# A Perceiver-style block: the values product of the self-attentions over both batches of a tile at once

## The reference

```python
# mla: q and k through Gelu and rotation, causal; ffn: not causal; attn: causal
scores = jnp.einsum('bhqd,bhkd->bhqk', q, k) * scale
attn   = jax.nn.softmax(scores, axis=-1)
out    = jnp.einsum('bhqk,bhkd->bhqd', attn, v)      # the values product
x      = x + out.reshape(b, s, E) @ wo               # (+ bo)
```

## Time and profile before

| what | value |
|---|---|
| median of 3 runs | 1062.91 us (1062.78 to 1072.04) |
| span of the profiled execution, first to last instruction | 1060.4 us |
| median less that span | 2.5 us |
| TensorE busy | 1019.5 us, 96% |
| VectorE, ScalarE, GpSimd busy | 647.4, 469.6, 243.5 us |
| self-attentions with values products | 362 to 513 us and 900 to 971 us |

### The profile page before, as it was taken

The page is one execution under the profiler, slowest core; times in us unless marked ns, Lnnn a source line. Parts: engine busy times, 40 slices in busy tenths (PEclk is TensorE's granted clock), DMA queues, the critical chain, the costliest instruction groups (busy, mean ns, idle before and its releaser), DMA issues.

```text
span 1060.4 us, 27662 instructions
## 1 busy us (share of the span) xinstructions
PE 1019.5 (96%) x11767; PEld 879.2 (83%) x11767; DVE 647.4 (61%) x1399; ACT 469.6 (44%) x863; POOL 243.5 (23%) x381
## 2 busy tenths in 40 slices
PE   5999999999999999999899999997999999999998
PEld 5888888888888787887689999996888888887887
DVE  5645645545333555776869999986667663355242
ACT  3333333333333556543156677762534433464232
POOL 2311211211111133442414444422211100011000
PEclk9999999999999999999889999999999999999999
DMA  9400000000000630220136557612111002000000
GB/s 306 140 2 21 21 2 21 2 1 1 2 1 2 227 123 3 81 101 13 43 79 239 198 199 257 239 61 90 41 38 47 12 2 72 3 2 2 1 20 20
DMA packets 55401, 72.54 MB, mean 68 GB/s; under 512 B 8488, under 2 KB 48624, under 8 KB 54640
## 3 DMA queue, kind: packets, MB, share of 16 engines
q1 hardware_dynamic: 53744, 66.59, 18.8%
q0 software_dynamic: 1536, 4.20, 1.3%
HBM read 59.76 MB, written 11.01 MB: 67 GB/s over the span
## 4 chain that ended last, share of the span: by engine, by line
PE 87%; DVE 7%; ACT 3%; issue 2%; DMA 1%; POOL 0%; DVEq 0%; ACTq 0%; POOLq 0%
PE ps L624 9%; PE ps L639 9%; PE ps L2321 8%; PE ps L2337 7%; PE ps L2684 5%; PE ps L1512 4%; PE ps L608 3%; PE ps L656 3%; PE ps L1430 3%; PE ps L1146 3%; PE ps L578 3%; PE ps L676 2%; PE ps L1469 2%; PE ps L1529 2%; PE ps L1081 2%; PE ps L1071 2%
## 5 line engine op out<-in xcount | busy, mean ns | idle before, releaser
L379 POOL TENSOR_TENSOR rn_tmp<-rn_cur,eps 128x1 f32<-128x1 f32 x48 | 14.1, 294 | 358.9 <-DVE rn_cur L373 358.7
L767 ACT ACTIVATE x0pT<-ps 128x512 f32<-128x512 f32 x64 | 38.3, 598 | 123.6 <-PE ps L639 123.6
L2321 PE MATMUL ps<-moe_xT_hi,ew_1hi 128*128 128x256 f32 x240 | 69.9, 291 | 2.3 <-DVE moe_xT_lo L2471 2.3
L2337 PE MATMUL ps<-ew_2hi,eh_hi 128*128 128x256 f32 x240 | 69.3, 289 | 2.5 <-DVE eh_lo L2479 2.5
L2321 PE MATMUL ps<-moe_xT_lo,ew_1hi 128*128 128x256 f32 x240 | 69.0, 288 | 0.0
L2321 PE MATMUL ps<-moe_xT_hi,ew_1lo 128*128 128x256 f32 x240 | 69.0, 287 | 0.0
L2477 DVE CAST eh_hi<-eh 128x512 fp32r<-128x512 f32 x60 | 61.1, 1018 | 11.0 <-ACT eh L2383 10.9
L2337 PE MATMUL ps<-ew_2hi,eh_lo 128*128 128x256 f32 x240 | 67.0, 279 | 0.0
L2337 PE MATMUL ps<-ew_2lo,eh_hi 128*128 128x256 f32 x240 | 66.9, 279 | 0.0
L876 DVE TENSOR_TENSOR x0A_lo<-ps,x0A_hi 128x512 fp32r<-128x512 f32 x64 | 41.1, 685 | 31.7 <-ACT x0A_hi L758 31.7
L2684 PE MATMUL ps<-f,ffw 128*128 128x512 f32 x256 | 59.1, 391 | 0.8 <-issue 0.6
(11 more groups left out here) (340 smaller groups left out, 2846.2 us busy)
## 6 DMA issues: line engine op xcount, KB each, us to landing
ew<-L_ffn_W_dram SPq DMA_DIRECT2D x30, 1024.0 KB, 7.2
x0cin<-ctx_dram SPq DMA_DIRECT2D x8, 512.0 KB, 4.2
x1cin<-ctx_dram SPq DMA_DIRECT2D x8, 512.0 KB, 4.0
moe_out<-moe_y SPq DMA_DIRECT2D x15, 256.0 KB, 7.8
xg<-moe_in SPq DMA_DIRECT2D x14, 256.0 KB, 7.8
moe_in<-padneg SPq DMA_DIRECT2D x3, 1024.0 KB, 12.4
maskrow<-mask_BxS_ik_dram SPq DMA_DIRECT2D x2, 1024.0 KB, 8.2
x0wk<-L_xattn_Wkv_dram SPq DMA_DIRECT2D x1, 1024.0 KB, 7.7
```

The lines of the kernel that those rows point to most:

```text
L767: nc.scalar.activation(g.pT[:, u, :], ps[:, S_BANK[u % 2], :], ACT.Exp, scale=64.0 ** -0.5).then_inc(C0.exp, 1)
L2321: last = nc.tensor.matmul(ps[:, n % 3, j * BT:j * BT + BT], w[b % 2][:, i, f * P:f * P + P], v[b % 2][:, i, :], start=(i == 0 and m == 0), ...
L2337: last = nc.tensor.matmul(ps[:, O_BANK[b % 2] + c, 0:D], v[n % 3][:, j * BT + c * P:j * BT + c * P + P], w[b % 2][:, f, :], start=(f == 0 ...
```

## The change

The values of an item lie in g.v as a block diagonal: for each head 2 x 18 columns, in which the keys of batch b fill only the columns of block b, and the other block holds zeros. One matmul then takes all 128 partitions of pT (both batches' keys) and 36 columns. Its output has the 64 queries of the head on 64 partitions, and both batches beside each other in the columns. The two halves of the output partitions hold heads j and 8 + j in place of the two batches. An item has 16 such matmuls, in two halves of 8. The zeros and ones come from a small tile "frame", filled once by VectorE and copied by GpSimd into the three buffers of v before each stage; the copies of v out of PSUM become two instructions of 64 partitions, and wait for that. The reciprocals, the scaled result and the transposed copy follow the new order of heads. Since v is larger, ln_st, hot_too and one eh_lo buffer lie elsewhere.

```diff
+        frame = sb("frame", [P, 2 * XVW])
...
-            v = [sb(f"sa_v{i}", [P, H, XVW]) for i in range(3)]
+            v = [sb(f"sa_v{i}", [P, H, 2, XVW]) for i in range(3)]
...
@@ self_tables(dve), in the first cross-attention
+            for b in range(2):
+                half = slice(64 * b, 64 * b + 64)
+                nc.vector.memset(frame[half, (1 - b) * XVW:(1 - b) * XVW + XVW], 0.0)
+                nc.vector.memset(frame[half, b * XVW:b * XVW + 16], 0.0)
+                last = nc.vector.memset(frame[half, b * XVW + 16:b * XVW + XVW], 1.0)
+            last.then_inc(SA.frame, 1)
@@ pool_x0(pool), loop over t and u
                     clip(t, u)
+                    if t == T - 1 and u == 4:
+                        value_frame(pool)
@@ pe_self
-            def fill_pv(n, hf):
-                if hf == 0:
+            def fill_pv(n, half):
+                if half == 0:
                     pe.wait_ge(SA.exp, n + 1)
+                    pe.wait_ge(SA.v_frame, 3 * span + 3)
                     RS.wait_emptied(pe, n, "v")
                     RS.wait_free(pe, n, "pv")
-                for hd in range(8 * hf, 8 * hf + 8):
-                    r, par = hd // 2 % 4, hd % 2
-                    for b in range(2):
-                        rows_b = slice(64 * b, 64 * b + 64)
+                for j in range(4 * half, 4 * half + 4):
+                    r, par = divmod(j, 2)
+                    for hf in range(2):
                         at_p = hf * P + par * N
-                        last = nc.tensor.matmul(RS.bank(n, "pv")[rows_b, hd * XVW:hd * XVW + XVW], g.pT[rows_b, r, at_p:at_p + N], g.v[n % 3][rows_b, hd, :],
-                                                start=True, stop=True, skip_group_check=True)
-                if hf == 1:
+                        last = nc.tensor.matmul(RS.bank(n, "pv")[64 * hf:64 * hf + 64, 2 * j * XVW:2 * j * XVW + 2 * XVW], g.pT[:, r, at_p:at_p + N],
+                                                g.v[n % 3][:, 8 * hf + j, :, :].rearrange("p b d -> p (b d)"), start=True, stop=True, skip_group_check=True)
+                if half == 1:
                     last.then_inc(SA.fill, 1)
@@ act_self (and the same on VectorE in dve_self)
             def v(n):
                 RS.wait_filled(act, n, "v")
-                nc.scalar.activation(g.v[n % 3][:, :, 0:16], RS.bank(n, "v")[:, 0:D].rearrange("p (h d) -> p h d", h=H), ACT.Copy).then_inc(SA.by_act, 1)
+                act.wait_ge(SA.v_frame, 3 * span + 3)
+                for b in range(2):
+                    half = slice(64 * b, 64 * b + 64)
+                    last = nc.scalar.activation(g.v[n % 3][half, :, b, 0:16], RS.bank(n, "v")[half, 0:D].rearrange("p (h d) -> p h d", h=H), ACT.Copy)
+                last.then_inc(SA.by_act, 1)
@@ attT(n)
-                bank = RS.bank(n, "T")
+                bank = RS.bank(n, "T")[:, 0:D].rearrange("p (b k n) -> p k b n", b=2, k=KD)
+                attT_b = g.attT[:, :, :].rearrange("p k (b n) -> p k b n", b=2)
...
-                    last = nc.scalar.activation(g.attT[:, :, :], bank[:, 0:D].rearrange("p (k n) -> p k n", k=KD), ACT.Copy)
+                    last = nc.scalar.activation(attT_b, bank, ACT.Copy)
@@ self_begin
-            for i in range(3):
-                nc.vector.memset(SB.v[i][:, :, 16:XVW], 1.0)
@@ attend(n)
-                nc.vector.reciprocal(g.rinv[:, :], pv[:, :, 16]).then_inc(SA.rinv, 1)
+                nc.vector.reciprocal(rinv, pv[:, :, :, 16]).then_inc(SA.rinv, 1)
                 dve.wait_ge(SA.rinv, n + 1)
-                nc.vector.tensor_tensor(g.att[:, :].rearrange("p (h d) -> p h d", h=H), pv[:, :, 0:16],
-                                        g.rinv[:, :].rearrange("p (h o) -> p h o", o=1).broadcast_to((P, H, 16)), ALU.mult).then_inc(SA.by_dve, 1)
+                nc.vector.tensor_tensor(g.att[:, :].rearrange("p (b j d) -> p j b d", b=2, j=8), pv[:, :, :, 0:16],
+                                        g.rinv[:, :].rearrange("p (j b o) -> p j b o", b=2, o=1).broadcast_to((P, 8, 2, 16)), ALU.mult).then_inc(SA.by_dve, 1)
@@ new, called by pool_x0 and pool_x1
+        def value_frame(pool):
+            pool.wait_ge(SA.frame, 1)
+            for i in range(3):
+                nc.gpsimd.tensor_copy(SB.v[i][:, :, :, :].rearrange("p h b d -> p h (b d)"),
+                                      frame[:, :].rearrange("p (o e) -> p o e", o=1).broadcast_to((P, H, 2 * XVW))).then_inc(SA.v_frame, 1)
```

More of the change, by code:

```diff
@@ L99, in build @@
         wg = sb("wg", [P, KD, P])
-        ln_st = sb("ln_st", [P, 5, 6])
         ln_mv = sb("ln_mv", [P, 5, 2])
@@ L178, in build @@
             wo = sb("x0wo", [P, 8, D])
+            ln_st = sb("ln_st", [P, 5, 6])
         at[0] = mark
@@ L215, in build @@
         b2 = sb("b2", [P, D])
-        eh_lo_at = at[0]
-        eh_lo = [sb("eh_lo2", [P, 512], F32R)]
         hot = [nc.alloc_sbuf_tensor_at(f"hot{i}", [P, BT], F32, offset=o) for i, o in enumerate(
-            [xg_at + 4 * D * i for i in (0, 1, 2, 3, 4, 5, 8, 9, 10, 11)])]
-        hot_too = nc.alloc_sbuf_tensor_at("hot_too", [P, BT], F32, offset=eh_lo_at)
+            [xg_at + 4 * D * i for i in (0, 1, 2, 3, 4, 5, 8, 9)])]
+        hot_too = nc.alloc_sbuf_tensor_at("hot_too", [P, BT], F32, offset=xg_at + 4 * D * 10)
         slot_no = nc.alloc_sbuf_tensor_at("slot_no", [P, BT], F32, offset=xg_at + 8 * D * 3)
@@ L226, in build @@
         eh_hi = [sb(f"eh_hi{i}", [P, 512], F32R) for i in range(3)]
-        eh_lo = [sb(f"eh_lo{i}", [P, 512], F32R) for i in range(2)] + eh_lo
+        eh_lo = [sb(f"eh_lo{i}", [P, 512], F32R) for i in range(3)]
         assert at[0] <= u_at
@@ L304, in ln_statistics @@
             for i, src in enumerate(srcs[done:]):
-                last = nc.vector.bn_stats(ln_st[:, done + i, :], src)
+                last = nc.vector.bn_stats(X0.ln_st[:, done + i, :], src)
             last.then_inc(ln_stats, 1)
@@ L309, in ln_statistics @@
             for i in range(len(srcs)):
-                last = nc.vector.bn_aggr(ln_mv[:, i, :], ln_st[:, i, :])
+                last = nc.vector.bn_aggr(ln_mv[:, i, :], X0.ln_st[:, i, :])
             last.then_inc(ln_aggr, 1)
@@ L443, in build @@
             ready = sem("sa_ready")
+            frame = sem("sa_frame")
+            v_frame = sem("sa_v_frame")
             roped0 = sem("sa_roped0")
@@ L1780, in attT @@
                 RS.wait_filled(act, n, "T")
-                bank = RS.bank(n, "T")
+                bank = RS.bank(n, "T")[:, 0:D].rearrange("p (b k n) -> p k b n", b=2, k=KD)
+                attT_b = g.attT[:, :, :].rearrange("p k (b n) -> p k b n", b=2)
                 if ITEMS[n][0] == "mla":
                     for k in range(KD):
-                        last = nc.scalar.activation(g.attT[:, k, :], bank[:, k * P:k * P + P], ACT.Identity, bias=vec("bv0", k))
+                        last = nc.scalar.activation(attT_b[:, k, :, :], bank[:, k, :, :], ACT.Identity, bias=vec("bv0", k))
                 else:
-                    last = nc.scalar.activation(g.attT[:, :, :], bank[:, 0:D].rearrange("p (k n) -> p k n", k=KD), ACT.Copy)
+                    last = nc.scalar.activation(attT_b, bank, ACT.Copy)
                 last.then_inc(SA.by_act, 1)
@@ L1897, in v @@
                 RS.wait_filled(dve, n, "v")
-                nc.vector.tensor_copy(g.v[n % 3][:, :, 0:16], RS.bank(n, "v")[:, 0:D].rearrange("p (h d) -> p h d", h=H)).then_inc(SA.by_dve, 1)
+                dve.wait_ge(SA.v_frame, 3 * span + 3)
+                for b in range(2):
+                    half = slice(64 * b, 64 * b + 64)
+                    last = nc.vector.tensor_copy(g.v[n % 3][half, :, b, 0:16], RS.bank(n, "v")[half, 0:D].rearrange("p (h d) -> p h d", h=H))
+                last.then_inc(SA.by_dve, 1)
             def k(n):
```

5 lines of the change are left out of this document (3 added, 2 removed).

## The result

The changed kernel takes 1050.07 us (median; 1047.72 to 1055.44, 4 runs) against 1063.09 us for the kernel before on the same chip, a ratio of 0.987 [0.983, 0.992]. Forecast were 1044.5 us and the range 1039 to 1052: the direction and the range hold, and the gain is 13.0 us where 18.6 were forecast. The profiled execution is the longest of the four, 1055.44 us with a span of 1053.7 us. Run again, the same kernel took 1047.36 us in six runs (first experiment) against 1063.69 us for the kernel before in the same rounds, 16.3 us less, and its trace is the better measure of the change.

A forecast was written before the change was run, and what follows sets the result against it. TensorE was taken as the bound, with the values product on its path. Of 25.7 us removed, 19.1 would arrive, less 0.34 and 0.1 for copies: 18.6 us saved, giving 1044.5 us; range 1039 to 1052.

The forecast's parts named there:

- What bounds the kernel: TensorE, busy for 96% of the span; the self-attentions' values product (L1512) is on the path, with VectorE waiting in 20 of 24 items.
- The main term: Values product: 32 records for 64 an item at 31.2 ns each, saving 1.07 us an item, 25.7 us over 24 items.
- Above 40 ns a record the forecast fails: Sign for the values product at L1512: 768 records of 128*64 with 36 columns, halves of 0.50 us.
- If items 16 to 23 gain less than 8 us, my reading of the free engines is wrong: Sign for the last stage, where eight items were to save 1.07 us each, 8.6 us.
- Row halves: Values product: records of the two batches in different row halves follow every 32.5 ns, so they give no second record at once.
- rival (c): Values product: the row halves do overlap, so nothing is saved and 0.44 us is added, 1063.3 us; chance 0.03.
- Items 1, 3, 5 and 7: First stage, MLA item two ahead: ScalarE's chain starts after the first half alone, so each saves 0.54 us, 2.2 together.
- Items 6, 8 and 10: First stage: VectorE's negation is slow beside GpSimd's weight split, so each saves only about 0.2 us, 0.6 together.
- Item 14: First stage: counted among seven items where VectorE waits over a microsecond for the product, so saving the full 1.07 us.
- The copies: Second copy of v per item: 0.34 us lost on VectorE at the first item, about 0.1 us in all on ScalarE.
- GpSimd's passes: Two passes laying zeros and ones in v, 2.3 us each, both hidden at no cost; up to 4 us once if uncovered.
- The clock: Low-clock stretch from 520 to 530 us behind the routing: shifts of 2 to 3 us either way; large case, chance 0.03.

The follow-up runs named there:

- first experiment: The changed kernel run again with no edit, six runs and one trace: 1047.36 us, ratio 0.985 to the kernel before.

## Why the prediction was right or wrong

**What bounds the kernel: right.** The product was on the path. In the last stage four steps are shorter by just what the product's groups are shorter, 2 x (1.04 - 0.59) = 0.90 us, and the others by 0.83 to 0.88; no other engine takes the place of TensorE. Doubling the records gives the old period back.

**The main term: mechanism right, size off.** The step that failed is "36 columns should cost 31.2 ns: a half of 16 records 0.50 us", with the sentence that changing the array's shape between groups costs nothing new. I divided groups of 64 records by their count and took the quotient as the price of a record. It holds two terms, 0.029 us a record and about 0.11 us for a group that borders on another shape; the second does not shrink with the count. The rows had it: 64 records in 1.98 us and 32 in 1.04 give 0.94 / 32 = 0.029 and 0.10. I read the difference between 30.9 and 32.5 ns as one between shapes. It was one between counts. A half takes 0.59 us, an item saves 0.90 and not 1.07 (2.08 - 1.00 is 1.08; the 1.07 is a slip of 0.01); over the 14 items with no other limit this is 2.4 us of the 4.4 that are missing (18.6 forecast, 14.2 found). The bounds of 30.9 and 31.6 ns, "under 0.4 us in all", were bounds of the wrong quantity. That the range of 1039 to 1052 us held is owed to the terms it was made for, the clock and the copies; it had none for this.

**The signs that were named.** "Above 40 ns a record the forecast fails" didn't say how a record is counted: busy time gives 41.4 ns, starts 36.9. "If items 16 to 23 gain less than 8 us, my reading of the free engines is wrong": they gained 7.0, and yet the reading stands, since no step there waits for a free engine. 8 x 0.90 is 7.2 us, so this sign tested the main term over again.

**Row halves.** That 64-row tiles gain nothing by working beside each other at 18 columns stands, by a better comparison than mine: both shapes cost 0.029 us a record, and 32 records take 1.04 and 1.06 us. The rule of the Trainium skill that I set as rival (c) (TensorEngine Tiling (Array Packing), section Tiling Modes: tiles multiply in parallel; its section Overview, Theoretical Speedup: up to twice the speed) is not what the trace shows here. The section Tiling Modes also says, under its key properties, that changing the tiling mode drains TensorE. With this the trace agrees: 0.1 us on either side of a full-array group between tiled ones, 0.30 and 0.32 us for an item with two changes fewer. What TensorE does in that time no row shows. I had read past it, since the changes were there before as well; but what is there before and after in full is just what a saving by quotient must leave out.

**Items 1, 3, 5 and 7: right**, 2.02 us for 2.2, by ScalarE's chain that moves with the first half alone; with both halves behind its start they give 0.49 us more each. TensorE waits 0.29 us for the transposed copy at item 5 and 0.26 at item 7, 0.53 and 0.54 at items 1 and 3.

**Items 6, 8 and 10: right**, 0.49 us for 0.6, and the cause is shown: with GpSimd's split moved away from VectorE's negation they give 2.26. The transposes wait 0.41 to 0.61 us, where 0.7 to 0.9 were named.

**Item 14: wrong.** I put it among the items that save in full by its wait for the product alone. Its halves have between them a group that waits for VectorE, which I had not looked at. Items 14 and 15 together were to give 1.3 us and gave 0.37, with a shorter low stretch in that.

**The copies: half right.** Nearly all are hidden, as forecast. The one at item 0 cost 0.56 us for 0.34: I took the distance from a copy to what follows, 0.34 us, for the price of one more, and two copies take 0.90. Item 4 lost 0.23 us on ScalarE's copy, where "a few hundredths each" were foreseen; items 6, 8 and 10 have VectorE as their limit and show none. **GpSimd's passes: half right.** The first costs nothing, in the gap that was named. The second was put at nothing because GpSimd had time for it; what it lies beside was not asked, and VectorE's norm there takes 0.26 us longer. **Order of heads, buffers, waits:** nothing showed.

**The clock.** Two or three us either way were named for the stretch behind the routing; in the second execution it gave at most 0.8 us back behind the first expert. Not foreseen was another low stretch at the steps of items 0 and 1, in three of the ten traces, one of them of a kernel without the change, worth 1.7 to 4.4 us each. It may be why the first four runs have their median at 1050 and six later ones at 1047: the mean clocks fit, 0.982 to 0.989 in the three slower of the four, 0.990 to 0.993 in the four faster of the six. Where the clock was low only the profiled execution of each shows. What starts it in one execution and not in the next stays open.

## What to carry to other kernels

Fit a line through groups of the same shape and different counts before pricing "half the records": here 0.029 us a record and 0.11 us a group, and the second term stays. Full-array groups and groups of smaller shapes are best ordered so that they alternate seldom; joining two halves gave 0.3 us an item, a third of what the merging gave, by moving calls alone. And for each place where a saving is counted, look at what stands between the parts that get shorter, not only at who waits at the end. Work that is added to an idle engine has a price if it runs beside a step that others wait for: look at what it lies beside, as at GpSimd's split and at its second pass.

## What was not expected of the hardware

A full-array group of 8 records between two tiled groups takes 1.09 us and 16 take 1.98, so 0.111 us a record and 0.20 us for the two sides; a group of 2 between full-array neighbours takes 0.22 us, with no such term. Records of 128 rows with 36 columns and of 64 rows with 18 columns cost the same 0.029 us. In execution after execution of nearly the same program the low clock comes at 369, 368 or 370 us or not at all, and lasts 3.4, 6.8 or 10.3 us; a saving of 2 us can only be read from the items' own steps, not from a span or a single time.
